# A decoder layer on one core: the order of the attention steps written out letter by letter

## What is computed

```python
x = x + _L0_attn_ref(_layernorm(x, axis=-1), L0_attn_w_qkv, L0_attn_w_out)
x = x + _L0_xattn_ref(_layernorm(x, axis=-1), ctx_1024, ctx_1024, mask_SxS2_ik0, ...)
x = x + _L0_ffn_ref(_layernorm(x, axis=-1), L0_ffn_clip_x, L0_ffn_clip_down, ...)
# attention, in both kinds
scores = jnp.where(mask, scores / sqrt(16), -jnp.inf)
out = jnp.einsum('bhqk,bhkd->bhqd', softmax(scores), v)
# feed-forward
scale = jax.nn.sigmoid(clip_factor) * jnp.max(jnp.abs(x)) / QMAX
```

## Time and profile before

| | |
|---|---|
| median of 3 runs | 784.86 us (781.35 to 786.49) |
| the profiled execution: its own time | 788.43 us |
| its span, first to last instruction | 786.4 us |
| attention part | up to about 672 us |
| feed-forward part | about 114 us |
| TensorE (PE) busy in the span | 657.6 us, 84% |
| VectorE (DVE), ScalarE (ACT), GpSimd (POOL) busy | 516.0, 410.9, 162.4 us |

### The profile page before, as it was taken

How to read it: one execution, slowest core, us unless ns; L and a number is a source line. 1 busy time by engine, 2 the same in 40 slices (tenths; PEclk the granted TensorE clock), 3 DMA queues, 4 the chain that set the end, 5 groups by cost and what they waited for, 6 DMA issues and landing times.

```text
span 786.4 us, 19952 instructions
## 1 busy us (share of the span) xinstructions
PE 657.6 (84%) x8015; PEld 409.8 (52%) x8020; DVE 516.0 (66%) x985; ACT 410.9 (52%) x602; POOL 162.4 (21%) x213
## 2 busy tenths in 40 slices
PE   3788999899989988999999888997978884487575
PEld 2556575666555655576566544665545433233254
DVE  6578567768755476676468663667546804589867
ACT  3244756546575446644645454442431461599693
POOL 4002222203132303200313121020030000145400
PEclk9889999999999998999999799999877557699879
DMA  8633343225341344253324324423361121000014
GB/s 246 168 108 120 98 110 114 58 72 163 113 115 35 118 131 121 61 161 98 67 83 135 106 46 110 123 52 87 75 201 50 23 52 35 0 1 1 0 57 158
DMA packets 58553, 72.16 MB, mean 92 GB/s; under 512 B 23979, under 2 KB 35423, under 8 KB 58463
## 3 DMA queue, kind: packets, MB, share of 16 engines
q1 hardware_dynamic: 54783, 68.92, 31.2%
q10 hardware_dynamic: 3680, 1.97, 1.0%
HBM read 17.74 MB, written 4.72 MB: 29 GB/s over the span
## 4 chain that ended last, share of the span: by engine, by line
PE 52%; DVE 20%; issue 7%; DMA 7%; ACT 6%; SPq 5%; ACTq 1%; POOL 1%; DVEq 0%; POOLq 0%
PE banks L665 34%; PE banks L845 5%; DVE mneg L1277 4%; PE banks L765 4%; PE banks L856 3%; SPq L598 2%; DVE tops L1456 2%; DMA oc<-sums 2%; ACT big L1081 2%; SPq L593 2%; PE banks L709 1%; DVE xn L1242 1%; PE banks L910 1%; DVE big L1450 1%; DMA big<-kparts 1%
## 5 line engine op out<-in xcount | busy, mean ns | idle before, releaser
L665 PE MATMUL banks<-big 96*128 96x77 bf16 (+3 forms) x1344 | 173.4, 250 | 22.2 <-issue 6.1
L1081 ACT ACTIVATE big<-banks 128x1024 f32<-128x1024 f32 (+1 forms) x128 | 122.7, 974 | 77.6 <-PE banks L665 65.2
L1277 DVE TENSOR_REDUCE mneg<-banks 128x4 f32<-128x896 f32 (+3 forms) x128 | 126.7, 1015 | 49.5 <-PE banks L774 48.5
L665 PEld LDWEIGHTS banks<-big 99*128 99x128 bf16 (+2 forms) x1344 | 107.5, 107 | 90.6 <-issue 54.4
L1553 POOL TENSOR_SCALAR_AFFINE_SELECT big<-big 128x512 f32<-128x512 f32 x128 | 82.0, 641 | 338.6 <-ACT big L1081 337.7
L1085 ACT ACTIVATE big<-banks 77x1024 f32<-77x1024 f32 x64 | 64.7, 1019 | 71.4 <-PE banks L665 68.5
L665 PE MATMUL banks<-xnT,weights 128*128 128x512 f32 x192 | 90.7, 606 | 0.3
L1281 DVE TENSOR_REDUCE mneg<-banks 128x8 f32<-128x616 f32 x64 | 49.8, 793 | 52.8 <-PE banks L665 52.8
L845 PE MATMUL banks<-big 128*17 128x256 f32 (+1 forms) x1152 | 77.0, 352 | 2.3 <-POOL big L1553 1.9
L765 PE MATMUL banks<-big 96*32 96x160 bf16 (+3 forms) x1792 | 76.0, 268 | 2.8 <-DVE mneg L1277 2.4
L910 PE MATMUL banks<-oe,weights 128*128 128x512 bf16 x187 | 46.7, 393 | 10.8 <-DVE big L1450 4.4
(11 more groups left out here) (152 smaller groups left out, 1097.7 us busy)
## 6 DMA issues: line engine op xcount, KB each, us to landing
big<-parts SPq DMA_DIRECT2D x285, 128.0 KB, 2.4
oc<-sums SPq DMA_DIRECT2D x16, 512.0 KB, 4.5
oTs<-oe SPq DMA_DIRECT2D x64, 64.0 KB, 2.3
out_dram<-oTs SPq DMA_DIRECT2D x16, 256.0 KB, 2.2
xs<-in_x_dram SPq DMA_DIRECT2D x3, 1024.0 KB, 5.8
big<-oe SPq DMA_DIRECT2D x32, 64.0 KB, 2.3
oTx<-oe SPq DMA_DIRECT2D x32, 64.0 KB, 2.3
xs<-in_x_dram SPq DMA_DIRECT2D x2, 512.0 KB, 6.5
```

The lines of the kernel that those rows point to most:

```text
L665: return e.matmul(to[0:w], k[:, 0:w], q, start=start, stop=stop, skip_group_check=True)
L1081: e.activation(pt[u].rearrange("p (i n) -> p i n", i=4)[:, :, 0:n], pair(p).rearrange("p j (s n) -> p (j s) n", s=2)[:, :, 0:n], ACT.Exp, ...
L1277: e.tensor_reduce(M.rearrange("p (h c) -> p h c", h=4)[:, :, c], pair(p).rearrange("p j (s n) -> p (j s) n", s=2)[:, :, 0:160 + 32 * (c % 4)],
```

## The change

The list is no longer computed. `ORDER` has one letter for each of the 1295 steps, and `attention_order()` takes for each letter the next step of that letter's stream (`streams()`). The steps are the same 1295, and each engine has the same operations to do; the order is another on every engine. On TensorE 64 of 757 steps stand at the same place as before and a step moves by 4.7 places on average (at most 53); on VectorE by 9.3 of 570 (at most 78), on ScalarE by 2.9 of 458, on GpSimd by 2.4 of 169, in SyncE's queue by 1.3 of 156. Before, a few steps of `max`, `score` and `val` stood out of turn within their kind (`val` X1b 0 2 ahead of `val` X1b 0 1); now each kind runs in turn.

So that the statistics ahead of the feed-forward part can stand anywhere among the others on VectorE, they get a buffer of their own (`st3`, in a tile that is not in use then), and waits for what the order had guaranteed are written down: the first `max` of a turn waits for the `rows` of two turns back, `top3` for `out`, the first `top3` and `centre` for the last `end3`. All four are waits of VectorE for itself.

The diff, cut to its core (of the tables a few lines stand):

```diff
--- before.py
+++ after.py
@@ -30,157 +30,20 @@
 UNITS = {"s": NC, "x": 4}
 HALF_AT = {"s": 3, "x": 1}
 
-LENGTH = {"s": 23.07, "x": 9.8}
-PLACE = {"max s0s": (0.101, 0.552), "max s1s": (0.142, 1.062), "max s1x": (0.1, 1.583), "max x0x": (0.049, 0.655),
-         "max x1x": (-0.578, -0.299), "max x1s": (0.501, 1.408), "max s0s b": (0.833, 1.134),
...
-         "shift": (0.331, 2.181), "setup": (0.743, 1.329), "v first": (-1.962, -0.081), "qk first": (1.091, 2.415)}
-
-BEHIND = {"scaled": 4, "turned": 2, "scaled 4": 3, "split": 1, "vmove": 0, "bulk": 64, "turnm": 2, "evac": 3,
...
+ORDER = (
+    "fnlTTnnnRnnnnRNNnqzcqnncqqccAWnCfnMMVDVmmmmmmmmnqrmqtmBccqLmAcqnBCscnRsWDmMVsnmmFpvWVMsTNmmvvssNrqtv"
...
+    "mvmmmvrvyeyueusts5syvpiys5y5evepuuv5iv5ssxgdssyv5eeYv4v44vpgw5554xUoyyoyjgyojyyodjyJyYjJJ65pwJE")
...
+def streams():
+
+    layers = list(dict.fromkeys(j[0:2] for j in JOBS))
+    turns = [(job, g) for job in JOBS for g in range(2)]
+    own = [job for job in JOBS if job[0] == "s"]
+    blocks = [(job, z, blk) for job in JOBS for z in range(2 if job[0] == "s" else 1) for blk in range(2)]
+    units = [(job, g, j) for job, g in turns for j in range(UNITS[job[0]])]
+    turned = [layer + (c0,) for layer in layers for c0 in (0, 4)]
+    tiles = [(z, t) for z in range(3) for t in range(2 if z == 2 else FT)]
+    firsts = {
+        "m": [("max", job, g, c) for job, g in turns for c in range(0, NC, 1 if job[0] == "s" else 2)],
+        "r": [("rows", job, g) for job, g in turns],
+        "t": [("turnm", job, g) for job, g in turns],
+        "s": [("score",) + unit for unit in units],
+        "v": [("val", job, g, j, j == UNITS[job[0]] - 1) for job, g, j in units],
+        "e": [("evac", job, g, half) for job, g in turns for half in range(2)],
...
+    return {letter: iter(steps) for letter, steps in firsts.items()}
...
+    left = streams()
+    return [next(left[letter]) for letter in ORDER]
@@ -394,6 +211,7 @@
         small = sb("small", [128, 32], F32)
         amx = sb("amx", [128, 12], F32)
         tops = sb("tops", [128, 24], F32)
+        st3 = tops[:, 0:12].rearrange("p (a n) -> p a n", a=2)
         ext = sb("ext", [128, 2, NC], F32)
         wsc = sb("wsc", [128, 16], F32)
         winv = sb("winv", [128, 16], F32)
@@ -1273,6 +1091,8 @@
                     _, job, g, c = s
                     M = mneg[:, rows_n[job, g] % 2, :]
                     e.wait_ge(t_max, n_of[s])
+                    if c == 0 and rows_n[job, g] > 1:
+                        e.wait_ge(d_rows, 4 * (rows_n[job, g] - 1) - 2)
                     if job[0] == "s":
                         e.tensor_reduce(M.rearrange("p (h c) -> p h c", h=4)[:, :, c],
                                         pair(p).rearrange("p j (s n) -> p (j s) n", s=2)[:, :, 0:160 + 32 * (c % 4)],
@@ -1324,9 +1144,9 @@
                     _, b, c = s
                     t0, i = NC * b + c, c % 2
                     e.wait_ge(d_out, n_of["out", "x", b, c // 2 * 2])
-                    e.bn_stats(st[:, i, :], xs[:, t0, :]).then_inc(d_stat3, 1)
+                    e.bn_stats(st3[:, i, :], xs[:, t0, :]).then_inc(d_stat3, 1)
                     e.wait_ge(d_stat3, 2 * n_of[s] - 1)
-                    e.bn_aggr(mv[:, t0, :], st[:, i, :]).then_inc(d_stat3, 1)
+                    e.bn_aggr(mv[:, t0, :], st3[:, i, :]).then_inc(d_stat3, 1)
                 elif k == "root3":
                     b = s[1]
                     a, z = NC * b, NC * b + NC
@@ -1335,6 +1155,9 @@
                 elif k == "top3":
                     _, b, c = s
                     t0 = NC * b + c
+                    e.wait_ge(d_out, n_of["out", "x", b, c])
+                    if b and c == 0:
+                        e.wait_ge(d_end3, 3 * n_of["end3", b - 1])
                     for i, op in enumerate((ALU.max, ALU.min)):
                         e.tensor_reduce(ext[:, i, c:c + 2], xs[:, t0:t0 + 2, :], AX.X, op).then_inc(d_top3, 1)
                 elif k == "end3":
@@ -1353,6 +1176,8 @@
                     _, b, c = s
                     t0 = NC * b + c
                     e.wait_ge(d_stat3, 2 * n_of["stat3", b, c + 1])
+                    if c == 0:
+                        e.wait_ge(d_end3, 3 * n_of["end3", b - 1])
                     e.tensor_scalar(ext[:, 1, c:c + 2], mv[:, t0:t0 + 2, 0], -1.0, None, ALU.mult).then_inc(d_ctr, 1)
                 elif k == "far3":
                     _, b, c = s
```

More of the change, by code:

```diff
@@ L186, in root_of @@
 def root_of(kind, b, c):
     return ("root", kind, b, c // 4 * 4, c // 4 * 4 + 4) if (kind, b) == ("s", 0) else ("root", kind, b, 0, NC)
-def qk_steps(job):
-    return [("qk", job, z, blk) for z in range(2 if job[0] == "s" else 1) for blk in range(2)]
-def max_steps(p):
-    job, g = JOBS[p // 2], p % 2
-    return [("max", job, g, c) for c in range(0, NC, 1 if job[0] == "s" else 2)] + [("rows", job, g)]
-def out_steps(kind, b):
-    return [("force", "fin")] + [("out", kind, b, c) for c in range(0, NC, 2)]
@@ new lines, in streams @@
+def streams():
[13 more added lines that the diff above has]
+        "e": [("evac", job, g, half) for job, g in turns for half in range(2)],
+        "g": [("gather", job, g) for job, g in turns],
+        "p": [("spread", job, g) for job, g in turns],
+        "i": [("invert", job) for job in JOBS],
+        "d": [("store", job) for job in JOBS],
+        "w": [("widen", job) for job in JOBS],
+        "x": [("scale", job) for job in JOBS],
+        "o": [("out",) + layer + (c,) for layer in layers for c in range(0, NC, 2)],
+        "n": [("stats",) + layer + (c,) for layer in layers for c in range(NC)],
+        "R": [("root", "s", 0, 0, 4), ("root", "s", 0, 4, NC)] + [("root",) + layer + (0, NC) for layer in layers[1:]],
+        "N": [("scaled",) + part for part in turned],
+        "T": [("turned",) + part for part in turned],
+        "q": [("qk",) + block for block in blocks],
+        "c": [("split",) + block for block in blocks],
+        "A": [("bulk", job, 0, 0) for job in JOBS],
+        "B": [("bulk", job, 1, 0) for job in JOBS],
+        "C": [("bulk", job, 0, 1) for job in JOBS],
+        "D": [("bulk", job, 1, 1) for job in own],
+        "V": [("v", job, c0) for job in own for c0 in (0, 4)],
+        "M": [("vmove", job, c0) for job in own for c0 in (0, 4)],
+        "k": [("xkeys", job) for job in JOBS if job[0] == "x"],
+        "h": [("shift", b, c) for b in range(NB) for c in range(0, NC, 2)],
+        "y": [("stat3", b, c) for b in range(NB) for c in range(NC)],
+        "Y": [("root3", b) for b in range(NB)],
+        "u": [("top3", b, c) for b in range(NB - 1) for c in range(0, NC, 2)],
+        "U": [("end3", b) for b in range(NB - 1)],
+        "j": [("centre", NB - 1, c) for c in range(0, NC, 2)],
+        "J": [("far3", NB - 1, c) for c in range(0, NC, 2)],
+        "E": [("end4", NB - 1)],
+        "W": [("turnw", i, c) for i in range(4) for c in range(2)],
+        "K": [("turnc", b) for b in range(NB)],
+        "Q": [("masks",)],
+        "X": [("keys", f) for f in range(2)],
+        "L": [("xload", b) for b in (2, 3)],
+        "l": [("late loads",)],
+        "f": [("first ones", r) for r in (0, 1)],
+        "F": [("ones", r) for r in (2, 3)],
+        "z": [("clear",)],
+        "Z": [("mix",)],
+        "1": [("wload",)],
+        "2": [("wtop", z) for z in range(3)],
+        "3": [("wscale",)],
+        "4": [("wtile",) + tile for tile in tiles],
+        "5": [("wturn",) + tile for tile in tiles],
+        "6": [("wend",)],
+    }
+    return {letter: iter(steps) for letter, steps in firsts.items()}
```

166 lines of the change are left out of this document (11 added, 155 removed), and 57 rows, old and new, of tables (FINE, PLACE).

## The result

The changed kernel takes 704.9 us (median of four runs, 700.8 to 709.0) against 785.2 us: a ratio of 0.898 with a 95% interval of 0.892 to 0.905. Run again beside later kernels (new_again), it gave 708.2 us, 0.901 (0.896 to 0.905). The profiled execution took 700.8 us with a span of 698.7.

The account below looks back on a forecast made before the run. TensorE was taken to lose time to idle waits (59.1 us) and a low clock; 6.8 + 7 + 7 + 4 = 24.8 us off the profiled 788.43 gave 763.6, and 760 us as median; range 739 to 779.

Parts of the forecast that it names:

- Term C: TensorE's other waits, 37.4 us spread over many places: a fifth goes, 7 us (bounds -5 and 18).
- Term B: Stretch from the end of X2b to `out` x 2: reordered queue and more work between gain 7 us (bounds 2 and 10).
- Term A: TensorE's `turnm` waiting for the last `rows` operation: longer covers gain 6.8 us (bounds 3 and 9.7).
- Term D: TensorE's low clock from 612 to 645 us: 4 us gained (bounds -3 and 12.7).
- The new wait of 5 us: First `max` of X3b would wait about 5 us for its queries, where there was a wait of 2.6.
- 0.6 or more: Sign for Term D: granted clock in the 30 us before the last `val`; at 0.5 the term is nil.
- The clock comes back: Rival: the stretch from 612 us runs at 2.4 GHz, 41.5 us gained in all, 743 us; chance 0.20.
- The wait for `rows`: Sign in the new profile: TensorE's wait for the last `rows` operation at 6 us or less.
- idle time fell below 40: Sign: TensorE's idle time before 650 us falls from 59 to about 40 us.
- the slow rival: ScalarE's `evac` held up behind DMAs reading buffer `oe`: 810 us, mild form near 787; chance 0.07.
- The cost of `st3` and the added waits: The statistics' own buffer and VectorE's four added waits for itself were priced at nothing.
- the ends cancel to within 1 us: Order changes at the end of the attention part (`widen`, last `wturn`, `far3`) were to cancel within 1 us.

Follow-up runs that it names:

- old_order: Changed kernel with its buffer and added waits, but all 1295 steps in the order of before: 785.7 us, ratio 0.999 to the kernel before.
- val_later: Changed kernel with 46 `val` steps 1 to 8 places later: 725.4 us, ratio 0.920 to the kernel before.
- turnm_back: Changed kernel with `turnm` put back to 2 places behind `rows` in 24 of 32 turns: 736.9 us, other runs 754.5 to 758.4; no ratio given.
- old_warm2: As old_warm, with 8 more needless matmuls ahead of the last gap left (2.2 us at 613.6): 775.2 us, ratio 0.987 to the kernel before.
- turnm5: Kernel before with one number changed, `turnm` 5 places behind `rows` in place of 2: 809.5 us, ratio 1.029.
- rows_first: Changed kernel with `rows` directly behind the last `max` of its turn (30 of 32 turns): 707.9 us, ratio 0.902 to the kernel before.
- val_back: Changed kernel with 75 of 128 `val` put back directly behind the `score` two later: 712.8 us, ratio 0.907 to the kernel before.
- old_warm: Order of before with 47 needless matmuls in five TensorE waits between 578 and 613 us: 783.1 us, ratio 0.994 to the kernel before.

## Why the prediction was wrong

**Term C failed, by its base.** It said "59.1 less 12.6 less the 2.6, 3.4 and 3.1 of term B leaves 37.4 us" and gave a fifth of that. I had called the 59.1 us of idle time all that an order can take away. The ledger shows 168 us above the undisturbed price from 50 us on: it has the delays below some tenths of a us that are partly shown as busy time, and the matmuls that ran longer at the low clock. Less turnm (16.0), `out` x (18.1), `wturn` (5.6) and the clock of the end (9) that leaves 120 us. What A, B, D (below) and the part behind the last attention step (4) leave of the gain for C is 80 - 11 - 7 - 9 - 4 = 49 us, in place of 7. This is a remainder, good to some 8 us; no run has C alone.

Up to 14 us of the 49 are clock again: 14 us of undisturbed work was done at the low level between 50 us and the end of X2b before (9 in old_order), and none after (2 in new_again). That share wasn't measured by itself. Term C had no clock in it, and term D looked at 612 to 645 us alone.

My own count of covers had said "a third to a half fewer" waits, which of 120 us is 40 to 60. That the 49 us lie in it is luck as far as is shown, since val_later has fewer short covers still and is 17 us slower. Why the new order's many small delays are shorter, step by step, stays open. The discount to a fifth, for answers that wait in VectorE's queue, was too large for this order: `rows` takes 3.7 us in place of 3.1 (median) and costs little where `turnm` stands now, though 22 us where turnm_back puts it.

**Term A** was right in mechanism and too small: 11.0 us in the ledger for 6.8, above its upper bound of 9.7, which was idle time too. (Both are for all turns; I had counted two of them under B.) As idle time it was near (12.6 to 2.9). What I had not seen is that it is no term that stands alone: in the old order moving `turnm` alone to a later place costs 23 us, since `turnm` only divides the time between `max` and `score`. In the new order that time is longer as a whole (11.5 us in place of 8.8), and both answers fit in it.

**Term B** was right in size and in one of its two waits. `out` followed the last `val` by 22.2 us (21 to 23 forecast, 23.4 before), with 5.4 us more work between, 6.6 us in place of 7 forecast (reckoned as the forecast did; no run has B alone). The new wait of 5 us didn't come: the queue took 11.6 us from `wload` to the end of `parts`, as reckoned (12.3), but 13.6 us had passed on TensorE by then and not 10.4, in smaller waits of the steps between (1.16 and 0.56 us the largest).

**Term D** was the mis-sized one on the other side: 4 us, where the rival had 12.7 and old_warm2 measured some 9 in the old order; that the new order got the same 9 is an estimate. The clock was 0.99 from 535 to 560 us, the last 25 us before the last `val`, and 0.94 from 530 (0.6 or more was the mark). "Against it: a new wait of 5 us stands shortly before" was wrong, as that wait was. The rival "The clock comes back" was the nearest case, with its 743 us still 38 too high by term C.

**The other marks.** The wait for `rows` is below 6 us, as forecast; idle time fell below 40. ScalarE's `evac` (L912) waits as long as before (32 us in all, 31 before), 18 us of it for DMAs in place of 25, so the slow rival is out. The cost of `st3` and the added waits at nothing was right (old_order). That the ends cancel to within 1 us was not: the part behind the last attention step takes 117 us in place of 121.

## What to carry to other kernels

Idle time of the bounding engine doesn't bound what an order can give back: measure its steps from end to end against the fastest of their kind, price the difference, and ask how much of it is clock. Covers along one chain (`max`, `rows`, `turnm`, DMA, `score`) are to be counted as a sum and divided by the measured answers; moving one kind of step by a rule gained nothing in any of five experiments here (turnm5, turnm_back, rows_first, val_back, val_later), and cost from nothing (rows_first) to 50 us (turnm_back). And needless matmuls in the waits put a price on the clock, once they leave no gap ahead of the stretch (old_warm2, not old_warm).

## What was unexpected in the hardware

In these traces the clock of a stretch doesn't follow from how busy TensorE is in it. From 616 to 645 us, with the same order of steps, it was 0.51 with TensorE busy 27.8 of 29 us (old_warm) and 0.84 with it busy 15.9 of 29 (old_warm2), where the matmuls were also shorter because the clock was up. What the kernels differ in is a gap of 2 us ahead of the stretch, which old_warm2 fills with 8 needless matmuls; in old_warm it stands at 613.9, and the clock fell at 616.6:

```profile
613.64 0.30 PE L768 MATMUL banks<-maskq,identb 128*128 128x308 bf16 x1
615.83 0.38 PE L768 MATMUL banks<-big 99*77 99x256 bf16 x2 [1.89 <-ACT weights L1219]
```

Once down, the clock stayed down through the dense work to 645 us and the waits behind it, 41 us in old_warm and 48 us in the kernel before. "TensorE: Matmul & The Clock Gate" in the Trainium skill (Part 1) says that activity releases the throttle; in these traces 27.8 of 29 us shown as busy didn't.
